# A third shared-expert product ahead of the output projection, and a one-column copy behind the expert choice

## The chip, the cores and the metric

The kernel runs on one core of one Trainium2 chip. The metric is device time in microseconds (us) of one execution. A core has TensorE (PE, matrix products; its weight loads are shown apart as PEld), VectorE (DVE), ScalarE (ACT), GpSimd (POOL) and SyncE (SP), each with an instruction stream of its own that runs strictly in order. Engines wait for each other only through semaphores.

## The reference, cut to what matters

4096 tokens of 256 channels go through an RWKV block and then through a layer of experts.

```
xk, xv, xr = xn*mix + shift(xn)*(1-mix)          # xn: layer norm, shift: one token back
k, v, r    = xk@Wk.T, xv@Wv.T, xr@Wr.T
x   = x + (sigmoid(r) * wkv(k, v)) @ Wo.T        # wkv: running sums over the tokens
xn2 = layer_norm(x); xk2, xr2 = mixed and shifted likewise
x   = x + sigmoid(xr2@Wr_ffn.T) * (relu(xk2@Wk_ffn.T)**2 @ Wv_ffn.T)
...
idx = argmax(xf @ Wg)                            # one of 8 experts for each token
out = geglu(xf, w1s, w2s, w3s) + geglu(xf, W1[idx], W2[idx], W3[idx])
```

`geglu(x, a, b, c)` is `(gelu(x@a) * (x@b)) @ c` with 1024 inner channels. Layer norms and residual sums stand around both parts.

## The kernel before, in words

The tokens go through in 16 chunks of 256. `chunk_steps` runs a software pipeline: step `i` works on chunk `c0 = i` (time mix: k, v, r, the scans, the output projection), `c1 = i-1` (channel mix), `c2 = i-2` (shared expert and expert choice), `c3 = i-3` (shared expert's down projection, placing and sending the rows), and prepares the inputs of chunk `i+1`. Steps -1 to 5 are written out, steps 6 to 13 come from a loop of two steps a turn, steps 14 to 17 are written out again. After them a second phase, `slot_steps`, takes the tokens sorted by expert in slots of 128; the change does not touch it.

What sets the order inside a step is the order in which each engine's `step` function calls its helpers (all in `build`). Four places matter here.

**TensorE's `step`** (lines 588 to 618) ends with `channel_mix_down(0..3)`, `output()`, `shared_gate(2)`, `shared_up(2)`, `shared_gate(3)`, `shared_up(3)`; the next step opens with `projection(0)`, `projection(1)`, `transpose_normed2()`. `output()` (L562) waits for `rw`, the product `val*er` that VectorE writes in L1099. `shared_gate(g)` forms `xf@w1s` for a quarter of the inner channels in PSUM bank `up[(3+2g)%4]`; for `g = 2` it waits for the split of `xf` and for `relu_up(0)`. Each shared product, and each of the three projections, is `channel_major`: 12 half-precision products of 256 columns (a value is split in a high and a low half, and `three` at L342 to L344 adds three partial products). The fp32 products (L546, L549, L562) are each recorded as two instructions.

**VectorE's `step`**, in its middle: `shared(0)`, `shared(1)` (L1207, each waits for ScalarE and for `shared_up`), in every odd step the low half of an expert's weights (`late_lo`, L983), `den_old`, `num_old`, `den_now` (L1070, L1089, L1074), then `halo` (L1002), `own(0)`, `gate` (L1154 to L1162), then `den_r` (L1079), `num` (L1094), `mix0` (L1012), `divide` (L1084), `rw` (L1099).
- `halo(xnT, i+1, ...)` copies the last token's column of this chunk's `xnT` in front of the next chunk's. It waits for ScalarE's `xnT_norm` (L663), and GpSimd's `delta_of` (L1507) waits for it.
- `own(0)` does anything in step 2 alone: the low half of the last weight piece (L977, 2048 elements a partition).
- `gate(c2)` takes the 8 logits of each token, their maximum and its index, casts the index and compares it to get a one-hot row.
- `mix0` needs `delta`, so it waits for GpSimd.

**GpSimd's `step`** runs `delta_of()`, then `mix_lo(0)`, `mix_lo(1)` (L1560), `sh_lo(0)` (L1554), `scatter(c3)` (two indirect DMAs), `sh_lo(1)`, `mix_lo(2)`, `inverse2()` and `inverse1()` (L1466 to L1476). `mix_lo(m)` waits for ScalarE's `mix_hi(m)` (L785), which waits for `mix0(m)`.

**The way from the output projection to the next step:** `x2_sum` (L1106, waits for `output()`), `x3_moments` and `x2_moments` (L989, L992) on VectorE, `inverse2` and `inverse1` on GpSimd, `ln2` on ScalarE (L669, behind `gelu(3)`, a table load and `sh_hi(2)`), and then `transpose_normed2()` on TensorE (L351).

Of the kernel before, what the change touches and what calls it, by code (L numbers as in the profile page):

```python
# [38 lines left out]
def wait(eng, sem, value):  # L39


    if not isinstance(value, int) or value > 0:
        eng.wait_ge(sem, value)


def build(nc, a):
    ctx = ExitStack()
    with ctx:
        def sb(name, shape, dt=F32):
            return ctx.enter_context(nc.sbuf_tensor(name, [P] + list(shape), dt))  # L50
# [6 lines left out]
        def S(name):  # L57
            if name not in sems:
                sems[name] = ctx.enter_context(nc.semaphore(name))
            return sems[name]  # L60
# [45 lines left out]
        xnT = [sb(f"xnT{b}", [CT, CH + 1]) for b in range(2)]  # L106
# [121 lines left out]
        def on(c):  # L228

            return not isinstance(c, int) or 0 <= c < NC  # L230

        def at_step(i, n):
            return isinstance(i, int) and i == n
# [113 lines left out]
        def _(pe):  # L347
# [55 lines left out]
            def step(i, p, h):  # L403
# [67 lines left out]
                def shared_of(g, mat, bank, done):  # L471
                    channel_major(bank, lambda j, s, k: shared_w[:, mat, s, k * F + (2 * g + j) * P:
                                                                 k * F + (2 * g + j + 1) * P], xf_s, done)

                def shared_gate(g):
                    if not on(c2):
                        return
                    if at_step(i, 2) and g == 0:
                        pe.wait_ge(S("piece_lo"), NEEDS_SHARED)
                    wait(pe, S("xf_lo"), c2 + 1)  # L480

                    if g >= 2:
                        if on(c1):
                            wait(pe, S("relu"), 4 * c1 + 2 * g - 3)
                        else:
                            wait(pe, S("gelu"), PAIRS * c2 + g - 1)
                    elif g == 0:
                        if on(c2 - 1):
                            wait(pe, S("gelu"), PAIRS * c2 - 1)
                        else:  # L490
                            wait(pe, S("relu"), 4 * c1 - 3)
                    elif on(c0):
                        wait(pe, S("val"), c0 + 1)
                    else:
                        wait(pe, S("gelu"), PAIRS * c2)
                    shared_of(g, 0, up[(3 + 2 * g) % 4], "sh_gate_mm")

                def shared_up(g):
                    if not on(c2):
                        return  # L500

                    if g >= 2:
                        if on(c1):
                            wait(pe, S("relu"), 4 * c1 + 2 * g - 2)
                        else:
                            wait(pe, S("gu"), PAIRS * c2 + g - 1)
                    elif on(c0):
                        wait(pe, S(("dist", "er")[g]), c0 + 1)
                    else:
                        wait(pe, S("gu"), PAIRS * c2 + g - 1)  # L510
                    shared_of(g, 1, up[(4 + 2 * g) % 4], "sh_up_mm")
# [25 lines left out]
                def channel_mix_down(q):  # L537
                    if not on(c1):
                        return
                    if at_step(i, 1) and q == 0:  # L540
                        pe.wait_ge(S("fv_in"), 16)
                    if q == 0:
                        wait(pe, S("y_sh"), c1 - 1)
                    wait(pe, S("kf"), 4 * c1 + q + 1)
                    for f in (2 * q, 2 * q + 1):
                        pe.matmul(yp[1][:, 0, :], kf[:, f, 0:P], w_fv[:, f, :], start=(f == 0), stop=(f == FT - 1))  # L546
                    if q == 3:
                        for f in range(FT):
                            m = pe.matmul(yp[1][:, 1, :], kf[:, f, P:CH], w_fv[:, f, :], start=(f == 0),  # L549
                                          stop=(f == FT - 1))  # L550
                        m.then_inc(S("fv_mm"), 1)

                def output():
                    if not on(c0):
                        return
                    if at_step(i, 0):
                        pe.wait_ge(S("o_in"), 16)
                    wait(pe, S("rw"), c0 + 1)
                    wait(pe, S("sig"), c0)
                    for t in range(TT):  # L560
                        for k in range(CT):
                            m = pe.matmul(yp[0][:, t, :], val[:, k, t * P:(t + 1) * P], w_o[:, k, :], start=(k == 0),  # L562
                                          stop=(k == CT - 1))
                    m.then_inc(S("wo_mm"), 1)
# [46 lines left out]
                    ranks(c2)  # L611
                for q in range(4):
                    channel_mix_down(q)
                output()
                shared_gate(2)
                shared_up(2)
                shared_gate(3)
                shared_up(3)
# [3 lines left out]
                if at_step(i, NC) or at_step(i, NC + 1):  # L622
                    for q in range(PAIRS + 1):
                        shared_down(c2, q)

            chunk_steps(pe, step)

            pe.wait_ge(S("y_sh"), NC)
# [331 lines left out]
        def _(dve):  # L960
            def held(sem, value):

                wait(dve, sem, value)
                if not isinstance(value, int):
                    dve.memset(hold_dve[:], 0.0)
# [32 lines left out]
            def halo(buf, c, b, done, norm):  # L998

                wait(dve, S(norm), CT * (c + 1))  # L1000
                last = 0 if isinstance(c, int) and c == 0 else CH
                dve.tensor_copy(buf[b][:, :, 0:1], buf[1 - b][:, :, last:last + 1]).then_inc(S(done), 1)  # L1002
# [69 lines left out]
            def den_now(c):  # L1072
                wait(dve, S("denominator"), 4 * c + 1)
                dve.tensor_tensor(den[:], den[:], ex[:, E_NOW], ALU.add).then_inc(S("denominator"), 1)  # L1074

            def den_r(c):
                wait(dve, S("denominator"), 4 * c + 2)
                wait(dve, S("er"), c + 1)
                dve.scalar_tensor_tensor(out=er[:], in0=er[:], scalar=1.0, in1=den[:], op0=ALU.add,  # L1079
                                         op1=ALU.mult).then_inc(S("denominator"), 1)  # L1080
# [10 lines left out]
            def num(c):  # L1091
                wait(dve, S("old"), c + 1)
                wait(dve, S("now"), c + 1)
                dve.tensor_tensor(val[:], now[:], dist[:], ALU.add).then_inc(S("num"), 1)  # L1094
# [53 lines left out]
            def gate(c):  # L1148

                CHOICE = 2 * TT + 1  # L1150
                logit = tp[0][:, 0, 0:TT * E].rearrange("p (t e) -> p t e", t=TT)
                held(S("gate_mm"), c + 1)
                for t in range(TT):
                    dve.max(best[:, t, :], logit[:, t, :]).then_inc(S("choice"), 1)  # L1154
                held(S("choice"), CHOICE * c + TT)
                for t in range(TT):
                    dve.max_index(best_at[:, t, :], best[:, t, :], logit[:, t, :]).then_inc(S("choice"), 1)
                wait(dve, S("choice"), CHOICE * c + 2 * TT)
                dve.tensor_copy(best_f[:], best_at[:, :, 0]).then_inc(S("choice"), 1)
                wait(dve, S("choice"), CHOICE * (c + 1))  # L1160
                for t in range(TT):
                    dve.tensor_scalar(onehot[:, t, :], iota_e[:], best_f[:, t:t + 1], None,  # L1162
                                      ALU.is_equal).then_inc(S("onehot"), 1)
# [36 lines left out]
            def step(i, p, h):  # L1200
# [15 lines left out]
                def own(part):  # L1216
                    for n in own_pieces(OWN_LO, i, part):
                        own_lo(n)
# [57 lines left out]
                if on(c0):  # L1276
                    den_old(c0)
                    num_old(c0)
                    den_now(c0)
                if on(i + 1):  # L1280
                    halo(xnT, i + 1, 1 - p, "halo", "xnT")
                own(0)
                if on(c2) and not at_step(i, NC + 1):
                    gate(c2)
                if on(c0):
                    den_r(c0)
                    num(c0)
# [99 lines left out]
            def last_slots():  # L1387
# [13 lines left out]
                dve.tensor_copy(slot_expert[:], slot_f[:, EXPERT, :]).then_inc(S("slot_table"), 1)  # L1401

            chunk_steps(dve, step)

            def slot_step(j, b, h):
# [284 lines left out]
```

## Time and profile before

| | |
|---|---|
| time, median of 3 runs | 1024.32 us (1023.39 to 1027.34) |
| the profiled execution's own time | 1025.26 us |
| its span | 1023.5 us |
| PE busy | 932.7 us, 91% |
| DVE busy | 719.4 us, 70% |
| ACT busy | 587.0 us, 57% |
| POOL busy | 587.9 us, 57% |
| granted TensorE clock, mean | 0.97 |
| two steps of the middle of the chunk phase | 75.2 us (output projections at 301.68 and 376.84) |

An instruction's row gives its start and duration in microseconds from the start of the span, and in brackets how long its engine had been idle before it and what ended that. Busy shares are means over stages with different limits: in the chunk phase (up to about 660 us) VectorE is busy some nine tenths of the time, in the slot phase it is less. The ends of matmuls are modelled, and matmuls overlap, so that distances between their starts say more than their durations.

### The profile page before, as it was taken

The page shows a single profiled execution, that of the slowest core. Times are in us where ns is not written, and L with a number is a line of the kernel's source. Part 1 is how long each engine was busy: PE and PEld are TensorE (multiplying, and loading weights), DVE is VectorE, ACT ScalarE, POOL GpSimd, SP SyncE. Part 2 cuts the span into 40 slices and gives each one's busy share as a digit, 9 for nine tenths or more (in the row PEclk, how much of TensorE's full clock was granted, in tenths as well). Part 3 has the DMA queues.
Part 4 walks back from the last instruction along what each step waited for, and adds up shares of the span by engine and source line. Part 5 has one row for each costly group of instructions (what it writes and reads, how often), then busy time and mean ns, then how long its engine had stood idle before and what let it go on. Part 6 is the DMA issues. An engine that isn't in the chain of part 4 may idle for free.

```text
span 1023.5 us, 28050 instructions
## 1 busy us (share of the span) xinstructions
PE 932.7 (91%) x9734; PEld 839.7 (82%) x9734; DVE 719.4 (70%) x1653; ACT 587.0 (57%) x1014; POOL 587.9 (57%) x800
## 2 busy tenths in 40 slices
PE   2387899999999999999999999779999999999994
PEld 1266789888888888888888878568999999999994
DVE  6988898998998998998998984513444444444442
ACT  5477677778768868868868755223333333333331
POOL 5446567767766766866866542434445554545553
PEclk9688999999999999999999999889999999999998
DMA  7113151351352252152161268375886788476510
GB/s 236 62 53 112 44 185 50 118 206 34 113 208 56 88 205 81 63 212 96 41 231 68 84 206 285 135 238 194 289 263 216 238 271 261 154 257 195 183 54 22
DMA packets 87338, 156.36 MB, mean 153 GB/s; under 512 B 5549, under 2 KB 68142, under 8 KB 82160
## 3 DMA queue, kind: packets, MB, share of 16 engines
q1 hardware_dynamic: 35760, 72.74, 20.8%
q10 hardware_dynamic: 46960, 65.89, 19.9%
q0 software_dynamic: 4560, 16.98, 4.3%
q8 instruction: 33, 0.54, 0.2%
q14 instruction: 25, 0.20, 0.1%
HBM read 178.35 MB, written 50.51 MB: 224 GB/s over the span
## 4 chain that ended last, share of the span: by engine, by line
PE 60%; DVE 17%; issue 8%; ACTq 6%; ACT 4%; POOL 2%; DMA 2%; DVEq 0%; POOLq 0%
PE up L342 12%; PE up L344 12%; PE up L343 12%; PE yp L342 6%; PE yp L343 6%; PE yp L344 6%; DVE er L1084 5%; PE yp L562 3%; ACTq L881 2%; DVE mixed L1012 2%; PE tp L351 1%; DVE arena L983 1%; DVE val L1099 1%; ACTq L901 1%; ACTq L884 1%
## 5 line engine op out<-in xcount | busy, mean ns | idle before, releaser
L342 PE MATMUL up<-mix_s,arena 128*128 128x128 f16 x1248 | 211.2, 219 | 3.6 <-DVE ex L1426 2.1
L343 PE MATMUL up<-mix_s,arena 128*128 128x128 f16 x1248 | 211.1, 219 | 0.0
L344 PE MATMUL up<-mix_s,arena 128*128 128x128 f16 x1248 | 211.1, 219 | 0.0
L342 PE MATMUL up<-xf_s,arena 128*128 128x256 f16 x512 | 140.3, 274 | 3.4 <-issue 2.4
L1655 POOL TENSOR_TENSOR kf_s<-ex,kf_s 128x512 f16<-128x512 f32 x78 | 90.2, 1156 | 88.5 <-ACT kf_s L942 88.4
L343 PE MATMUL up<-xf_s,arena 128*128 128x256 f16 x512 | 140.4, 274 | 0.0
L344 PE MATMUL up<-xf_s,arena 128*128 128x256 f16 x512 | 140.3, 274 | 0.0
L1426 DVE SCALAR_TENSOR_TENSOR ex<-up,ex 128x512 f32<-128x512 f32 x78 | 53.9, 691 | 105.0 <-ACT ex L936 104.7
L342 PEld LDWEIGHTS up<-mix_s,arena 128*128 128x128 f16 x1248 | 122.1, 98 | 5.3 <-DVE ex L1426 3.4
L343 PEld LDWEIGHTS up<-mix_s,arena 128*128 128x128 f16 x1248 | 122.1, 98 | 0.4
L344 PEld LDWEIGHTS up<-mix_s,arena 128*128 128x128 f16 x1248 | 122.1, 98 | 0.0
L1554 POOL TENSOR_TENSOR sh_s<-gu,sh_s 128x512 f16<-128x512 f32 x64 | 76.6, 1198 | 57.2 <-ACT sh_s L778 56.9
L936 ACT ACTIVATE ex<-up 128x512 f32<-128x512 f32 x78 | 45.9, 589 | 104.5 <-issue 54.0
L942 ACT ACTIVATE kf_s<-ex 128x512 f16<-128x512 f32 x78 | 49.1, 630 | 80.8 <-DVE ex L1426 68.7
L1560 POOL TENSOR_TENSOR mix_s<-mixed,mix_s 128x512 f16<-128x512 f32 x48 | 57.9, 1222 | 55.7 <-ACT mix_s L785 55.7
L342 PE MATMUL yp<-arena,kf_s 128*128 128x256 f16 x312 | 85.0, 273 | 0.8 <-issue 0.7
L343 PE MATMUL yp<-arena,kf_s 128*128 128x256 f16 x312 | 85.0, 273 | 0.0
L344 PE MATMUL yp<-arena,kf_s 128*128 128x256 f16 x312 | 85.0, 273 | 0.0
L342 PE MATMUL yp<-arena,sh_s 128*128 128x256 f16 x256 | 72.8, 284 | 10.4 <-POOL sh_s L1554 10.4
L771 ACT ACTIVATE gu<-up 128x512 f32<-128x512 f32 x64 | 36.8, 596 | 69.8 <-PE up L344 60.2
L343 PE MATMUL yp<-arena,sh_s 128*128 128x256 f16 x256 | 72.8, 284 | 0.0
L344 PE MATMUL yp<-arena,sh_s 128*128 128x256 f16 x256 | 72.5, 283 | 0.0
(228 smaller groups left out, 2893.8 us busy)
## 6 DMA issues: line engine op xcount, KB each, us to landing
arena<-w_split ACTq DMA_DIRECT2D x117, 1024.0 KB
arena<-in_W SPq DMA_DIRECT2D x24, 1024.0 KB, 6.2
w_split<-arena SPq DMA_DIRECT2D x24, 1024.0 KB, 9.1
rows<-routed_rows ACTq DMA_DIRECT2D x39, 261.0 KB, 2.9
routed_rows<-x_in SPq DMA_DIRECT2D x8, 650.0 KB, 6.3
normed<-routed_rows ACTq DMA_DIRECT2D x39, 128.0 KB, 2.5
x_in<-in_x SPq DMA_DIRECT2D x16, 256.0 KB, 2.8
x_res<-in_x SPq DMA_DIRECT2D x16, 256.0 KB, 2.8
```

The source lines that it names most:

```text
L342: pe.matmul(out, stat(0), mov(0), start=first, stop=False)
L343: pe.matmul(out, stat(0), mov(1), start=False, stop=False)
L344: return pe.matmul(out, stat(1), mov(0), start=False, stop=last)
L562: m = pe.matmul(yp[0][:, t, :], val[:, k, t * P:(t + 1) * P], w_o[:, k, :], start=(k == 0), stop=(k == CT - 1))
L771: act.activation(gu[g % GUS][:], up[(3 + 2 * g) % 4][:], ACT.Gelu, scale=1 / WS).then_inc(S("gelu"), 1)
L936: act.activation(slot_g[q], up[2 * q][:].rearrange("p k n -> p (k n)"), ACT.Gelu, scale=1 / WS).then_inc(S("slot_gelu"), 1)
L942: act.activation(slot_h[b][:, 0, q * FT // 2:(q + 1) * FT // 2, :], slot_g[q].rearrange("p (f n) -> p f n", n=P), ACT.Copy).then_inc(S("sl ...
L1084: dve.reciprocal(er[:], er[:]).then_inc(S("denominator"), 1)
L1426: dve.scalar_tensor_tensor(out=slot_g[q], in0=up[2 * q + 1][:].rearrange("p k n -> p (k n)"), scalar=HS / WS, in1=slot_g[q], op0=ALU.mult, ...
L1554: pool.tensor_tensor(sh_s[:, 1, 2 * g:2 * g + 2, :], gu[g % GUS][:], sh_s[:, 0, 2 * g:2 * g + 2, :], ALU.subtract).then_inc(S("sh_lo"), 1)
L1560: pool.tensor_tensor(mix_s[m][:, 1], mixed[m][:], mix_s[m][:, 0], ALU.subtract).then_inc(S("mix_lo"), 1)
L1655: pool.tensor_tensor(hs[:, 1], slot_g[q].rearrange("p (f n) -> p f n", n=P), hs[:, 0], ALU.subtract).then_inc(S("slot_h_lo"), 1)
```

## The change

On TensorE, `shared_gate(2)` moves from behind `output()` to ahead of it, in every step. On VectorE, `gate(c2)` and step 2's `own(0)` now come ahead of the `halo` of the next chunk. No instruction is added or removed, and the waits of the moved parts keep their values.

```diff
@@ TensorE, step
                 for q in range(4):
                     channel_mix_down(q)
+                shared_gate(2)
                 output()
-                shared_gate(2)
                 shared_up(2)
                 shared_gate(3)
                 shared_up(3)
@@ VectorE, step
                     den_now(c0)
-                if on(i + 1):
-                    halo(xnT, i + 1, 1 - p, "halo", "xnT")
                 own(0)
                 if on(c2) and not at_step(i, NC + 1):
                     gate(c2)
+                if on(i + 1):
+                    halo(xnT, i + 1, 1 - p, "halo", "xnT")
                 if on(c0):
                     den_r(c0)
                     num(c0)
```

On TensorE, at the end of a step (`yp<-w_o,val` is the output projection, `up<-xf_s,arena` a shared product; one group of three of the four stands for all):

```order
 L549 MATMUL yp<-w_fv,kf_s 128x256 x8
+L342 MATMUL up<-xf_s,arena 128x256
+L343 MATMUL up<-xf_s,arena 128x256
+L344 MATMUL up<-xf_s,arena 128x256
...
 L562 MATMUL yp<-w_o,val 128x256 x4
-L342 MATMUL up<-xf_s,arena 128x256
-L343 MATMUL up<-xf_s,arena 128x256
-L344 MATMUL up<-xf_s,arena 128x256
```

Twelve products now stand between the channel mix's last product and the output projection; as many fewer follow it before the next step.

On VectorE, in the middle of step 3 (`xnT<-xnT` is the halo's copy, `er<-er,mixed` is `den_r`):

```order
 L1089 TENSOR_TENSOR dist<-ex,state 128x512
 L1074 TENSOR_TENSOR mixed<-mixed,ex 128x512
-L1002 COPY xnT<-xnT 128x2
-L1154 MAX best<-tp 128x8 x2
-L1157 MAX_INDEX best_at<-best,tp 128x8 x2
-L1159 CAST best_f<-best_at 128x2
-L1162 TENSOR_SCALAR onehot<-iota_e,best_f 128x8 x2
+L1154 MAX best<-tp 128x8 x2
+L1157 MAX_INDEX best_at<-best,tp 128x8 x2
+L1159 CAST best_f<-best_at 128x2
+L1162 TENSOR_SCALAR onehot<-iota_e,best_f 128x8 x2
+L1002 COPY xnT<-xnT 128x2
 L1079 SCALAR_TENSOR_TENSOR er<-er,mixed 128x512
 L1094 TENSOR_TENSOR val<-mixed,dist 128x512
```

The copy now has two products of two SBUF tensors right behind it, where it had the small operations of the choice. In step 2 the weight split moves ahead of the copy as well:

```order
 L1074 TENSOR_TENSOR mixed<-mixed,ex 128x512
-L1002 COPY xnT<-xnT 128x2
 L977 SCALAR_TENSOR_TENSOR arena<-arena 128x2048
 L1154 MAX best<-tp 128x8 x2
```

There the copy stands behind both.

## Rows read from the trace of the kernel before

**Rows 1.** Waits of the whole span: us in total, times, longest.

```profile
PE yp L562 <- DVE val L1099: 21.5, 15, 10.4
```

**Rows 2.** TensorE in time around an output projection, an odd step (7).

```profile
293.81 3.62 PE L546 MATMUL yp<-w_fv,kf_s 128*128 128x256 f32 x16
297.27 3.62 PE L549 MATMUL yp<-w_fv,kf_s 128*128 128x256 f32 x16
301.68 1.99 PE L562 MATMUL yp<-w_o,val 128*128 128x256 f32 x8 [0.79 <-DVE val L1099]
...
311.38 0.65 PE L351 MATMUL tp<-ident,normed 128*128 128x128 f32 x4
```

**Rows 3.** The same in the even step behind it (8).

```profile
335.02 3.62 PE L549 MATMUL yp<-w_fv,kf_s 128*128 128x256 f32 x16
339.17 1.99 PE L562 MATMUL yp<-w_o,val 128*128 128x256 f32 x8 [0.54 <-DVE val L1099]
...
348.86 0.60 PE L351 MATMUL tp<-ident,normed 128*128 128x128 f32 x4
```

**Rows 4.** VectorE in time, odd step.

```profile
288.40 0.69 DVE L1207 SCALAR_TENSOR_TENSOR gu<-up,gu 128x512 f32<-128x512 f32 x1 [0.86 <-PE up L344]
...
293.02 0.16 DVE L1002 COPY xnT<-xnT 128x2 f32<-128x2 f32 x1
...
293.79 0.61 DVE L1159 CAST best_f<-best_at 128x2 f32<-128x2 uint32 x1
...
294.71 0.68 DVE L1079 SCALAR_TENSOR_TENSOR er<-er,mixed 128x512 f32<-128x512 f32 x1
...
295.92 1.67 DVE L1012 SCALAR_TENSOR_TENSOR mixed<-delta,vec,xnT 128x256 f32<-128x256 f32 x4
...
305.62 0.15 DVE L992 BATCH_NORM_AGGREGATE mv<-stats 128x2 f32<-128x6 f32 x1
```

**Rows 5.** VectorE in time, even step.

```profile
330.51 0.17 DVE L1002 COPY xnT<-xnT 128x2 f32<-128x2 f32 x1 [1.86 <-ACT xnT L663]
...
333.42 1.67 DVE L1012 SCALAR_TENSOR_TENSOR mixed<-delta,vec,xnT 128x256 f32<-128x256 f32 x4
```

**Rows 6.** GpSimd in time, odd step.

```profile
293.34 1.04 POOL L1507 TENSOR_TENSOR delta<-xnT 128x512 f32<-128x512 f32 x1 [4.47 <-DVE xnT L1002]
297.53 2.28 POOL L1560 TENSOR_TENSOR mix_s<-mixed,mix_s 128x512 f16<-128x512 f32 x2 [3.15 <-ACT mix_s L785]
...
306.08 0.20 POOL L1466 TENSOR_TENSOR inv<-mv,eps_ws 128x2 f32<-128x2 f32 x1
...
308.95 0.20 POOL L1476 TENSOR_TENSOR inv<-inv 128x2 f32<-128x2 f32 x1
```

**Rows 7.** ScalarE in time, odd step: ln2.

```profile
310.18 1.08 ACT L669 ACTIVATE normed<-x,inv 128x256 f32<-128x256 f32 x2
```

**Rows 8.** VectorE in time, step 15, where no halo stands ahead of the choice.

```profile
593.44 0.24 DVE L1154 MAX8 best<-tp 128x8 f32<-128x8 f32 x2
...
594.13 0.17 DVE L1159 CAST best_f<-best_at 128x2 f32<-128x2 uint32 x1
...
594.60 0.68 DVE L1079 SCALAR_TENSOR_TENSOR er<-er,mixed 128x512 f32<-128x512 f32 x1
```

**Rows 9.** GpSimd and VectorE in time where a small GpSimd operation lasts long.

```profile
318.14 4.16 POOL L1480 TENSOR_TENSOR inv<-inv,mv 128x2 f32<-128x2 f32 x1
...
321.56 0.68 DVE L1051 TENSOR_TENSOR dist<-ex,val 128x512 f32<-128x512 f32 x1
```

**Rows 10.** TensorE in time, step 2.

```profile
105.19 3.62 PE L549 MATMUL yp<-w_fv,kf_s 128*128 128x256 f32 x16
112.13 3.39 PE L562 MATMUL yp<-w_o,val 128*128 128x256 f32 x8 [3.33 <-DVE val L1099]
```

**Rows 11.** VectorE in time, step 2.

```profile
100.42 0.17 DVE L1002 COPY xnT<-xnT 128x2 f32<-128x2 f32 x1 [1.60 <-ACT xnT L663]
...
105.42 1.67 DVE L1012 SCALAR_TENSOR_TENSOR mixed<-delta,vec,xnT 128x256 f32<-128x256 f32 x4
```

## The prediction

> **What bounds the kernel now.** I began with TensorE's waits over the whole span. The row to see is the output projection waiting for VectorE's `val` (`rw`): 21.5 us in 15 waits [rows 1]. The longest, 10.4 us, is in step 0, where no shared product exists yet that could fill it; step 2 has 3.33 us [rows 10]; the rest, some 7.8 us, is spread over the twelve steps 3 to 14. Then I read TensorE in order of time around one such wait in each kind of step. Groups of 16 fp32 instructions follow each other at 3.46 us (293.81 to 297.27), so after the last group the next product could start at 297.27 + 3.46 = 300.73. It starts at 301.68: a **hole of 0.95 us** in the odd step [rows 2]. In the even step the same reckoning gives 338.48 against 339.17, **0.69 us** [rows 3]. TensorE has nothing else to wait for in these steps. So the chunk phase is bound by TensorE, plus this hole, whose length VectorE sets.
>
> VectorE itself is anchored to TensorE: it waits 0.86 us for `shared_up(1)` at 288.40 in the odd step [rows 4]. From there to `rw` it runs without a pause. In the even step it also waits 1.86 us at the halo for ScalarE's `xnT` [rows 5].
>
> **TensorE's part: twelve products into the hole.** A half-precision product of 256 columns takes a new place every 0.109 us: from the projection's start to the transposes there are 9.70 us (301.68 to 311.38 [rows 2]; 9.69 in [rows 3]), 72 products and the projection's own 1.83. Twelve are 1.31 us. After the change the projection can start 1.31 us after the free place and is followed by 9.70 - 1.31 = 8.39 us of work up to the transposes. If `rw` is ready by then, the whole hole goes: 0.95 us in an odd step, 0.69 in an even one. The data of the moved products (`xf`'s split, bank 3 after `relu_up(0)`) are old by then. Switching once more between fp32 and half precision I cost at nothing: from the half-precision products to the fp32 transposes the row shows no gap beyond the usual one.
>
> **VectorE's part: when is `rw` ready?** Before, the halo stands at 293.02, `delta` runs on GpSimd from 293.34 for 1.04 us beside the choice, `den_r` starts at 294.71 and `mix0` at 295.92 [rows 4, 6]. From halo to `delta` there are 0.32 us. The choice takes 1.61 us there (0.08 after the halo's start to 294.71), of which the cast is 0.61, and the cast ends at 294.40, just as `delta` does (294.38). In step 15, with no `delta` beside it, the choice takes 594.60 - 593.44 = 1.16 us and the cast 0.17 [rows 8]. So the cast waits for GpSimd, and moved ahead of the halo it won't.
>
> Now `delta` starts beside `den_r` and `num`, which both read two tensors from SBUF. What that does is bounded by two rows. Below, nothing: `delta` takes 1.04 us as now. Above, exclusion: a GpSimd operation on two numbers lasts from 318.14 to 322.30, 0.06 us after VectorE's product of two SBUF tensors that starts at 321.56 has ended [rows 9]. I take exclusion, because that row has the same kinds of operands. Then in an odd step:
> - choice 293.02 to 294.18, halo, `den_r` from 294.26 and `num` for 1.28 us in all, to 295.54. `delta` could start at 294.50, but gets through only then: to about 296.55.
> - `mix0` at 296.62 in place of 295.92: **0.70 us later**, and `rw` with it. It is ready 0.95 + 0.70 = 1.65 us after TensorE's free place; the moved products cover 1.31; a hole of 0.34 stays, and TensorE gains 0.61.
>
> The Trainium skill (page "SBUF — State Buffer", section "Who interferes with whom") has the rule: a VectorE instruction with two SBUF inputs and a GpSimd instruction that reads SBUF exclude each other, and whoever starts first keeps the port for the whole instruction. By its wording `delta` would slip in between `den_r` and `num`, where my row shows no slipping in; `mix0` would come out at 296.6 either way, so the sum is the same by both, and it speaks against this half of the change.
>
> In an even step the halo goes on waiting for `xnT` at 330.51, the choice fills that wait, `num` ends at 331.87 and `delta` about 332.9, some 0.5 us ahead of the 333.42 of before [rows 5]. `rw` is ready well before 1.31; TensorE gains its 0.69.
>
> **What is late next: the normed rows of the next step.** The projection comes later against TensorE's other work, and its result must go through VectorE's sums and moments, GpSimd's `inverse2` and `inverse1` and ScalarE's `ln2` before the transposes at 311.38, which have no slack: `ln2` ends at 311.26 [rows 2, 7]. But `ln2` now waits for ScalarE's own queue, which hangs on `shared_gate(3)` and so moves with TensorE: `inverse1` ends at 309.15 and `ln2` starts at 310.18 [rows 6, 7]. Less 0.08 for the signal, the slack is 0.95 us.
> - Odd step: ScalarE comes 0.61 us earlier. GpSimd's queue, which runs on from `mix_lo(0)` at 297.53 to `inverse2` at 306.08 and hangs on `mix0` [rows 6], comes 0.70 later. 1.31 - 0.95 = 0.36 short; gain 0.61 - 0.36 = **0.25 us**.
> - Even step: ScalarE 0.69 earlier; the projection 1.31 - 0.69 = 0.62 later. GpSimd's queue isn't late here; the moments were ready 0.31 us before `inverse2` began (305.77 against 306.08 [rows 4, 6], taken for the even step too) and 0.08 go to the signal, so `inverse2` starts 0.39 later. 1.08 - 0.95 = 0.13 short; gain **0.56 us**.
>
> Six pairs of steps, 3 to 14: 6 x 0.81 = **4.9 us**. A check on the size: the holes of [rows 2, 3] average 0.67 us by the waits' own count, the whole row 7.8/12 = 0.65.
>
> **Step 2.** Free place at 105.19 + 3.46 = 108.65, projection at 112.13: a hole of 3.48 us [rows 10]. VectorE was done at 100.42 - 1.60 = 98.82 and now does the weight split (2.20, 100.50 to 102.70 by the next instruction's start) and the choice (1.16) while it waited: halo 102.18, `num` to 103.46, `delta` to 104.5, `mix0` at 104.57 in place of 105.42 [rows 11]: 0.85 earlier. With 1.31 fewer behind the projection that is 2.16, less 0.13 as above. The projection took 3.39 us there and 1.99 elsewhere [rows 10, 2]: after this hole TensorE ran at the lower of its two clock levels. The new hole is 1.3 us, between one that leaves the clock alone (0.95) and one that does not (3.48); I take half of the 1.40. Together **2.7 us**.
>
> Steps 0 and 1 have no moved product, step 15 has no hole (its projection follows at once) and no halo, and nothing in the second phase is touched: 0. The halo's later place costs nothing to anyone but `delta`.
>
> Sum: 4.9 + 2.7 = 7.6 us off. Against the profiled execution, 1025.26 - 7.6 = 1017.7; that execution is 0.94 above the median of the runs shown, so 1024.3 - 7.6 = **1016.7 us**.
>
> **Rivals**, each by the same steps:
> - **No exclusion.** `delta` takes 1.04 us beside `den_r`. `mix0` comes 0.27 us earlier in odd steps; TensorE gains 0.95 - 0.13 = 0.82 there; pairs 8.3 us. Step 2: `mix0` at 103.6, 1.8 earlier, all the clock's 1.4 back: 4.5. About 1011.5 us. For it: nothing. Against it: the 4.16 us of [rows 9]. 0.10.
> - **The choice doesn't get shorter** (something else than `delta` held the cast): `mix0` 1.15 us later in odd steps, TensorE 0.16 earlier, 0.36 short: a loss of 0.20; pairs 6 x 0.36 = 2.2, step 2 about 2.2: 1019.9 us, no change that can be told. Against it: the matching ends. 0.18.
> - **The hole moves.** The slack of 0.95 us is not there and the wait for `rw` is paid again as a wait for the normed rows; step 2 alone gains: 1021.6 us. For it: the transposes start 0.12 us after `ln2` ends. 0.09.
> - **Slower: GpSimd's `inverse1` is held.** Later by 0.4 to 0.7 us, it falls deeper beside VectorE's `x1_sum`, two instructions of the shape of `mix0`, of which four take 1.67 us [rows 4]: 0.84 us. If its small operations are held that long, `ln2` and the transposes of `normed2` wait as much longer in 13 steps: 13 x 0.84 = 10.9 against the 7.6, 3.3 us slower, 1027.6 us. It turns the sign once the hold is over 7.6/13 = 0.58 us a step, and passes 0.5% at (7.6 + 5.1)/13 = 0.98; the hold of [rows 9], some 4 us, is the bound above. Against it: it stands beside that sum already. 0.07.
>
> **How the numbers follow.** The forecast has 0.56. Its own spread, some 2 us to either side from step 2's clock (0.7) and steps whose holes differ, puts nearly all of it below 1019.2. A measurement of this kernel can tell about 0.5% (5.1 us) from no change. Faster: 0.52 of the forecast and 0.10 of no exclusion, 0.62. Same: 0.34, with a part of the last rival. Slower: 0.04, the rest of it. The range 1011.5 to 1021.8 takes in all but that rival and tails.
>
> **What would show it.** Right: TensorE's waits at L562 in odd steps 0.2 to 0.4 us and none in even ones; the cast at 0.17 to 0.2 us; `delta` in odd steps recorded at about 2 us; two steps in 74.4 us in place of 75.2; small waits of L351 for `normed`. Wrong: `delta` at 1.04 us beside `den_r`, a cast of 0.6, or waits of L351 over 0.7 us a step.

## The result, and the profile after

The changed kernel takes 1010.96 us (median of 4 runs, 1010.42 to 1011.86), the kernel before 1023.86 us in the same comparison (1022.42 to 1027.34): ratio 0.987, 95% interval 0.9857 to 0.9884. That is 12.9 us less where 7.6 were forecast, and 0.5 us outside the range given (1011.5 to 1021.8). Sign and main mechanism were right, several sizes were not.

TensorE's waits over the whole span, after (us in total, times, longest), against the 21.5 us of [rows 1]:

```profile
PE yp L562 <- DVE val L1099: 11.7, 4, 10.4
```

Of the fifteen waits for `rw` four are left: step 0's of 10.4 us, step 2's of 0.96 and two small ones. The same three places in time as in [rows 2] and [rows 3], TensorE after, an odd step (7) and the even one behind it (8); the part between the rows is left out:

```profile
291.35 3.62 PE L549 MATMUL yp<-w_fv,kf_s 128*128 128x256 f32 x16
...
296.15 1.99 PE L562 MATMUL yp<-w_o,val 128*128 128x256 f32 x8
...
304.87 0.65 PE L351 MATMUL tp<-ident,normed 128*128 128x128 f32 x4 [0.18 <-ACT normed L669]
...
328.51 3.62 PE L549 MATMUL yp<-w_fv,kf_s 128*128 128x256 f32 x16
333.27 1.89 PE L562 MATMUL yp<-w_o,val 128*128 128x256 f32 x8
...
341.55 0.60 PE L351 MATMUL tp<-ident,normed 128*128 128x128 f32 x4
```

From one step's last channel-mix group to the next's there are now 37.16 us behind an odd step (before 37.75) and 36.62 behind an even one (365.13 - 328.51; before 37.42). The free place, where the next product could start, is 3.46 us after each L549. In the even step the projection starts 1.30 us after it, the length of the moved products, and the transposes follow 8.28 us later with no wait. In the odd step it starts at 296.15, 1.34 after the place, and the transposes come 10.06 after the place. Without a wait they would come at 9.72: 8.38 us behind a projection that had itself been waited for, as in step 2. That is a wait of 0.34 us for the normed rows, of which the row calls 0.18 idle.

VectorE after, the odd step's middle, against [rows 4]:

```profile
282.49 0.69 DVE L1207 SCALAR_TENSOR_TENSOR gu<-up,gu 128x512 f32<-128x512 f32 x1 [0.87 <-PE up L344]
...
287.80 0.17 DVE L1159 CAST best_f<-best_at 128x2 f32<-128x2 uint32 x1
...
288.28 0.16 DVE L1002 COPY xnT<-xnT 128x2 f32<-128x2 f32 x1
288.35 0.68 DVE L1079 SCALAR_TENSOR_TENSOR er<-er,mixed 128x512 f32<-128x512 f32 x1
288.95 1.53 DVE L1094 TENSOR_TENSOR val<-mixed,dist 128x512 f32<-128x512 f32 x1
290.40 1.66 DVE L1012 SCALAR_TENSOR_TENSOR mixed<-delta,vec,xnT 128x256 f32<-128x256 f32 x4
```

GpSimd and ScalarE after, the same step, against [rows 6] and [rows 7]:

```profile
288.60 1.33 POOL L1507 TENSOR_TENSOR delta<-xnT 128x512 f32<-128x512 f32 x1 [5.66 <-DVE xnT L1002]
...
303.42 0.20 POOL L1476 TENSOR_TENSOR inv<-inv 128x2 f32<-128x2 f32 x1
```

```profile
303.65 1.09 ACT L669 ACTIVATE normed<-x,inv 128x256 f32<-128x256 f32 x2 [0.22 <-POOL inv L1476]
```

The cast takes 0.17 us in all 16 steps. `delta` is recorded at 1.33 us and `num` at 1.53 instead of 0.68: `delta` asked while `den_r` ran, got through when `den_r` ended, and `num` stood until `delta` was done (289.93). `mix0` starts 7.91 us after `shared(1)`, before 7.52: 0.39 us later. And `ln2` in odd steps now waits for `inverse1`, where ScalarE's own queue had bound it.

VectorE after, the even step (8):

```profile
324.00 0.17 DVE L1002 COPY xnT<-xnT 128x2 f32<-128x2 f32 x1 [0.67 <-ACT xnT L663]
...
335.20 0.87 DVE L1106 SCALAR_TENSOR_TENSOR x<-normed,spread,yp 128x256 f32<-128x256 f32 x2 [1.10 <-PE yp L562]
```

The choice has eaten most of the 1.86 us of waiting at the halo [rows 5]. `x2_sum` (L1106) starts 1.93 us after the projection does (335.20 - 333.27).

Step 2, TensorE after, against [rows 10]:

```profile
105.88 3.62 PE L549 MATMUL yp<-w_fv,kf_s 128*128 128x256 f32 x16
111.77 2.00 PE L562 MATMUL yp<-w_o,val 128*128 128x256 f32 x8 [0.96 <-DVE val L1099]
```

Where the time went, from the starts of the rows of L549 in steps 2 and 15, of the second phase's first transposes (L377) and of the last store (L1647), us:

| | before | after | gain |
|---|---|---|---|
| up to step 2's last channel-mix group | 105.19 | 105.88 | -0.69 |
| step 2 to 3 | 41.90 | 37.85 | 4.05 |
| step 3 to 15 (12 intervals) | 450.16 | 442.22 | 7.94 |
| step 15 to the second phase | 74.06 | 74.44 | -0.38 |
| second phase | 343.51 | 340.92 | 2.59 |

The last row belongs to nothing in the change: in the twelve profiles of this study the second phase took 340.2 to 343.5 us, the part before it 72.4 to 75.6, the start 105.2 to 107.4, and none of the three goes with the kernel (three profiles of the changed kernel gave 74.4, 72.6 and 72.5 for the part before the second phase). The stretch from step 2 to step 15 repeats within 0.4 us in three profiles of the same program (480.07, 480.43, 480.04). So I judge the experiments by that stretch, "the chunk stretch", and use the medians as a check.

### The profile page after: what moved, and what is told of

Read it like the earlier page. It is cut to its first block, busy times and chain, and to the rows that moved or that the text cites. A ratio compares the mean times of both kernels' runs of the same rounds, so it can differ in the third digit from the quotient of the medians.

```text
span 1010.0 us, 28050 instructions
## 1 busy us (share of the span) xinstructions
PE 930.1 (92%) x9734; PEld 839.3 (83%) x9734; DVE 722.3 (72%) x1653; ACT 585.6 (58%) x1014; POOL 588.6 (58%) x800
## 4 chain that ended last, share of the span: by engine, by line
PE 69%; DVE 9%; issue 7%; POOL 7%; ACT 3%; DMA 2%; ACTq 1%; POOLq 0%; DVEq 0%
PE up L342 13%; PE up L344 13%; PE up L343 13%; PE yp L342 7%; PE yp L343 6%; PE yp L344 6%; PE yp L546 2%; PE yp L549 2%; PE yp L562 2%; PE tp L351 2%; DVE arena L983 1%; POOL mix_s L1560 1%; DVE er L1084 1%; POOL routed_rows L1595 1%; POOL sh_s L1554 1%
## 5 line engine op out<-in xcount | busy, mean ns | idle before, releaser
L344 PE MATMUL yp<-arena,sh_s 128*128 128x256 f16 x256 | 72.6, 284 | 0.0
```

The lines of the kernel that those rows point to most:

```text
L344: return pe.matmul(out, stat(1), mov(0), start=False, stop=last)
```

## The experiments

**e1: TensorE's half alone.**

```diff
--- before
+                shared_gate(2)
                 output()
-                shared_gate(2)
```

> TensorE's half of the change alone: the third shared gate ahead of the output projection, VectorE as before. Theory A (TensorE's half is nearly all of it, and in odd steps VectorE's half only costs): mix0 keeps its old place, rw is ready 0.95 us (odd) and 0.69 us (even) after TensorE's free place, both under the 1.31 us of the moved products, so both holes close; against the change the odd steps gain up to 0.35 us more each, while step 2 keeps a hole of about 2.2 us and perhaps the lower clock there. 6 x (0.95 + 0.80) = 10.5 us in steps 3 to 14, 1.3 to 2.7 in step 2: 11.5 to 13 us faster than the kernel before, about 1011 to 1012.5 us. Theory B (both halves are needed): with the halo in its old place even steps gain no more than 0.69 and odd ones stay at the change's 0.59, step 2 gives 1.3: about 9 us faster, 1015.

Measured: 1011.24 us, ratio to before 0.9872 (0.9851 to 0.9894). Chunk stretch 480.38 us against 492.06 before and 480.07 with the whole change. Steps 3 to 14: odd ones 36.63 to 36.89, even ones 36.62, both faster than or equal to the whole change. Step 2 to 3 takes 40.59 us, only the 1.31 of the moved products less than before:

```profile
106.82 3.62 PE L549 MATMUL yp<-w_fv,kf_s 128*128 128x256 f32 x16
113.77 3.33 PE L562 MATMUL yp<-w_o,val 128*128 128x256 f32 x8 [2.02 <-DVE val L1099]
```

Theory A holds. TensorE's half alone gives 11.7 of the chunk stretch's 12.0 us. VectorE's half on top of it gives 2.74 us in step 2 and loses 2.43 in the steps behind (442.22 against 439.79), 0.4 in each odd one.

**e2: VectorE's half alone.**

```diff
--- after
-                shared_gate(2)
                 output()
+                shared_gate(2)
```

> VectorE's half alone: choice and own split ahead of the halo, TensorE as before. Theory A: in odd steps mix0 comes 0.39 us later (the changed kernel's rows show it), the hole grows from 0.95 to 1.34 us; in even steps it comes 0.61 us earlier, the hole shrinks from 0.69 to about 0.1; pairs gain 0.2 us, step 2 gains 1.05 and what the clock gives back (up to 1.4). 2 to 4 us faster than the kernel before, 1020 to 1022. Theory B (VectorE's half is worth as much as TensorE's): 6 us or more.

Measured: 1022.38 us, ratio to before 0.9981 (0.9969 to 0.9993). Chunk stretch 489.46, 2.6 less than before, of it 2.73 in step 2. Even steps lose their hole entirely (the projection at +0.00; 36.74), that of odd steps from 7 on grows to 1.60 us and their interval to 38.41. That is more than the 1.34 expected. GpSimd, then VectorE, then TensorE in step 7 of this kernel:

```profile
294.02 1.93 POOL L1507 TENSOR_TENSOR delta<-xnT 128x512 f32<-128x512 f32 x1 [5.67 <-DVE xnT L1002]
```

```profile
294.37 0.68 DVE L1094 TENSOR_TENSOR val<-mixed,dist 128x512 f32<-128x512 f32 x1
296.06 1.67 DVE L1012 SCALAR_TENSOR_TENSOR mixed<-delta,vec,xnT 128x256 f32<-128x256 f32 x4 [1.01 <-POOL delta L1507]
```

```profile
301.82 1.99 PE L562 MATMUL yp<-w_o,val 128*128 128x256 f32 x8 [1.44 <-DVE val L1099]
```

Here `delta` did not slip in between: `num` ran its 0.68 us right behind `den_r` and `delta` was held over both, 1.93 us. The halo, `den_r`, `num` and `delta` start at the same distances as in the changed kernel, to 0.02 us. So the exclusion has two outcomes; what decides between them is not shown. Theory A's sum holds (2.2 us by the medians, 2.6 by the stretch), though the hole of odd steps grew by 0.65 us where 0.39 were expected.

**e3: halo ahead of the choice in odd steps, behind it in even ones.**

```diff
--- after
+                if on(i + 1) and p == 1:
+                    halo(xnT, i + 1, 1 - p, "halo", "xnT")
                 own(0)
                 if on(c2) and not at_step(i, NC + 1):
                     gate(c2)
-                if on(i + 1):
+                if on(i + 1) and p == 0:
                     halo(xnT, i + 1, 1 - p, "halo", "xnT")
```

> The changed kernel, but in odd steps the halo is back ahead of the choice; even steps (step 2 too) keep it behind. Theory A (the halo behind the choice costs in odd steps, because GpSimd's delta and VectorE's num exclude each other and GpSimd's queue behind it is late for inverse1): the wait for the normed rows at the transposes of odd-to-even steps (0.34 us) goes, six or seven of them: 2 us faster than the changed kernel, about 1009. Theory B (it costs nothing, since the moved products cover it): same as the changed kernel within 0.5 us, 1011.

Measured: 1011.71 us, ratio to before 0.987 (0.9849 to 0.9891), chunk stretch 477.75: 2.3 us below the changed kernel's. TensorE in step 7:

```profile
290.82 3.62 PE L549 MATMUL yp<-w_fv,kf_s 128*128 128x256 f32 x16
...
303.98 0.65 PE L351 MATMUL tp<-ident,normed 128*128 128x128 f32 x4
```

The transposes stand 9.70 us after the free place (290.82 + 3.46) in place of 10.06. `mix0` is back at its old place, 0.39 us earlier, and GpSimd's `inverse1` and the transposes come earlier by as much. Some 0.1 us of the wait is left: the transposes are 8.39 us behind the projection here, 8.28 in even steps. The stretch agrees with theory A, the median by itself did not show it, so it was run again (e10).

**e4: `shared_up(2)` ahead of the projection too.**

```diff
--- after
                 shared_gate(2)
-                output()
                 shared_up(2)
+                output()
```

> The changed kernel with shared_up(2) ahead of the output projection too, 24 products in place of 12. Theory A (the way from the projection through x2, the moments, inverse1 and ln2 to the next transposes has hardly any slack left): the projection comes 1.31 us later against TensorE's other work, ScalarE's ln2 can't start before inverse1, and each step waits at the transposes: 0.34 + 1.31 = 1.6 us in odd steps, about 1.1 in even ones, less what shared_up(2) had waited for: 12 steps, 13 to 16 us slower than the changed kernel, about 1025. Theory B (the slack is 0.95 us or more): 6 us slower or less.

Measured: 1023.78 us, ratio to before 0.9999 (0.9986 to 1.0012): the whole gain is gone. Chunk stretch 490.72, 10.65 more than the changed kernel's; intervals 37.87 behind odd steps (0.7 more) and 37.80 behind even ones (1.2 more). TensorE in step 7:

```profile
299.93 1.89 PE L562 MATMUL yp<-w_o,val 128*128 128x256 f32 x8
308.10 0.65 PE L351 MATMUL tp<-ident,normed 128*128 128x128 f32 x4
```

`ln2` waits 0.98 us for `inverse1` here, in odd and even steps, so this is the way from the projection to the normed rows at its bare length: 8.17 us, and 8.09 in the even step behind it. TensorE's own work on that way is 8.28 us after the change (the even step above) and 1.31 less here. So the changed kernel sits 0.1 to 0.2 us short of the point where the next product moved ahead costs its full length. This is nearer to A (13 to 16 us) than to B (6 or less): 10.65 us by the stretch, 12.8 by the medians. `delta` was held over both VectorE products in five of this kernel's six odd steps (1.93 us in step 7), as in e2.

**e5: the changed kernel again**, unedited.

> The changed kernel once more, unedited: is the way in which delta and num share the port in odd steps the same in another execution, and how much do the second phase and the start vary? Theory A (the outcome is fixed by the program's timing): delta 1.33 us and num 1.53 us in every odd step, intervals of 37.15 and 36.62 us between the last channel-mix products again, the chunk phase within 0.5 us of the first execution, the time about 1011, differences between executions in the start and the second phase alone (up to 3 us). Theory B (it falls either way by chance): some odd steps with delta at 1.93 and num at 0.68 us, whose intervals are about 0.3 us longer.

Measured: 1010.39 us, ratio 0.9884 (0.9866 to 0.9901), chunk stretch 480.43. All odd steps fall as before but one, step 5. GpSimd and VectorE there:

```profile
215.08 2.02 POOL L1507 TENSOR_TENSOR delta<-xnT 128x512 f32<-128x512 f32 x1 [5.92 <-DVE xnT L1002]
```

```profile
215.51 0.68 DVE L1094 TENSOR_TENSOR val<-mixed,dist 128x512 f32<-128x512 f32 x1
```

In the first execution that `delta` took 1.41 us and `num` 1.52. So the program alone doesn't fix the outcome: the same step of the same program falls either way, and it costs 0.27 us in that step (37.61 against 37.34). Mostly A, in one step B.

**e6: `den_r` ahead of the halo.**

```diff
--- after
+                if on(c0):
+                    den_r(c0)
                 if on(i + 1):
                     halo(xnT, i + 1, 1 - p, "halo", "xnT")
                 if on(c0):
-                    den_r(c0)
                     num(c0)
```

> The changed kernel with den_r ahead of the halo, so that num alone stands beside delta. Theory A (the port passes at an instruction's boundary): delta asks 0.32 us after the halo, when num has begun, and gets through when num ends: recorded at about 1.4 us, num at 0.68; mix0 comes 0.26 us later than in the changed kernel's odd steps, the projection starts 1.6 us after TensorE's free place there in place of 1.34; even steps, where the halo waits for xnT anyway, don't change. 1.5 to 2 us slower than the changed kernel. Theory B (two-input instructions keep the port as a run): delta runs when the run ends, as late as it would with both behind the halo: mix0 0.3 us later; the two differ by delta's length only. Theory C (no exclusion between these): delta 1.04 us, mix0 0.06 us earlier.

Measured: 1014.78 us, ratio to before 0.9919 (0.9901 to 0.9937); chunk stretch 481.85, 1.4 to 1.8 more than the changed kernel's. VectorE and GpSimd, step 7:

```profile
290.54 0.16 DVE L1002 COPY xnT<-xnT 128x2 f32<-128x2 f32 x1
290.61 0.69 DVE L1094 TENSOR_TENSOR val<-mixed,dist 128x512 f32<-128x512 f32 x1
292.31 1.67 DVE L1012 SCALAR_TENSOR_TENSOR mixed<-delta,vec,xnT 128x256 f32<-128x256 f32 x4 [1.01 <-POOL delta L1508]
```

```profile
290.87 1.33 POOL L1508 TENSOR_TENSOR delta<-xnT 128x512 f32<-128x512 f32 x1 [6.25 <-DVE xnT L1002]
```

`num` keeps its 0.69 us, `delta` is held until it ends and then takes the rest; `mix0` follows the halo by 1.77 us and the projection stands at +1.6 in odd steps (1.9 in step 5), as theory A had it. Even steps don't move. The median lies further off (3.8 us) than the stretch explains. The part from step 15 to the second phase took 1.7 us more here than in e5, but no more than in the changed kernel's first profile, so the rest is open.

**e7: step 2's weight split behind the halo.**

```diff
--- after
-                own(0)
                 if on(c2) and not at_step(i, NC + 1):
                     gate(c2)
                 if on(i + 1):
                     halo(xnT, i + 1, 1 - p, "halo", "xnT")
+                own(0)
```

> The changed kernel with step 2's weight split behind the halo again, the choice still ahead of it. Only step 2 can change. Theory A (the split ahead of the halo fills the wait for xnT, 1.6 us, which the choice fills by 1.2): in step 2 mix0 comes 0.6 to 0.9 us later than in the changed kernel (delta held beside the split), the projection starts about 3.2 us after TensorE's free place in place of 2.43, TensorE's hole grows to 1.9 us; if the clock stays up 0.8 us slower than the changed kernel, if it falls 2 us slower. All other steps the same. Theory B (the choice alone fills it): no difference in step 2.

Measured: 1010.9 us, ratio 0.9886 (0.987 to 0.9903). Step 2 to 3 takes 38.24 us, 0.39 more; the projection starts at +2.82. TensorE's hole is longer, and the clock stays up: windows of this kernel (stretch, us, busy by engine, PEclk, DMA):

```profile
108.00:116.00 8.00, 6.65 (x41) 5.48 (x40) 7.79 (x9) 6.48 (x8) 5.64 (x5) 1.00 0.00 0
```

Half of theory A's price: `delta` is recorded at 3.01 us beside the split, but `mix0` comes only 0.40 us later against TensorE than in the changed kernel, where 0.6 to 0.9 were expected. Moving the split ahead is worth 0.4 us, once.

**e8: `den_r` and `num` ahead of the halo**, so that `delta` runs beside nothing.

```diff
--- after
-                if on(i + 1):
-                    halo(xnT, i + 1, 1 - p, "halo", "xnT")
                 if on(c0):
                     den_r(c0)
                     num(c0)
+                if on(i + 1):
+                    halo(xnT, i + 1, 1 - p, "halo", "xnT")
```

> The changed kernel with den_r and num both ahead of the halo: nothing with two SBUF inputs stands beside delta. Theory A (exclusion costs 0.3 us in odd steps, and taking it away by waiting costs more than it gives): delta 1.04 us, num 0.68, mix0 0.53 us later than in the changed kernel's odd steps, the projection 1.87 us after the free place there; even steps unchanged or 0.3 us later in mix0, hidden; 3 to 4 us slower than the changed kernel. Theory B (the shared port is the larger cost): no slower.

Measured: 1013.41 us, ratio 0.9913 (0.9896 to 0.993), chunk stretch 483.73, 3.3 to 3.7 more than the changed kernel's; odd steps 37.5 to 37.8, the projection at +1.92 in most of them. GpSimd, step 7:

```profile
290.97 1.04 POOL L1507 TENSOR_TENSOR delta<-xnT 128x512 f32<-128x512 f32 x1 [6.88 <-DVE xnT L1002]
```

With neither product beside it `delta` is back at 1.04 us. So the 1.33 to 2.02 of the other kernels come from the two products. Waiting them out costs more than running beside them. The medians show 2.5 us of it, the stretch 3.3 to 3.7.

**e9 and e10: the changed kernel and e3's, side by side on one chip.**

> The changed kernel, to stand beside the next one on the same chip: about 1010.7 us; chunk phase 480.1 to 480.5 us from step 2's to step 15's last channel-mix products.

> Halo ahead of the choice in odd steps, behind it in even ones. In its first run this stretch took 477.75 us against the changed kernel's 480.07 in its own, but the medians of runs on different chips or hours did not show the 2.3 us. Theory A (the gain is real and was hidden by what varies in the start and the second phase): the stretch again 477.7 to 477.9 us, the median 1 to 3 us below the changed kernel's beside it. Theory B (it is given back behind the chunk phase): the stretch as before, the medians equal within 0.5 us, and the part behind step 15 longer by as much.

Measured: 1011.48 us (1009.35 to 1012.85) and 1009.13 us (1008.26 to 1010.89), ratios to before 0.9872 (0.9854 to 0.9891) and 0.9854 (0.9838 to 0.9871). Chunk stretches 480.04 and 477.71. The 2.3 us are real in the stretch and of that size in these medians too, but the intervals of the two ratios overlap, so the medians alone would not prove it. Theory B of e10 is not quite out: its profile took 2.1 us more from step 15 to the second phase (74.57 against 72.46), as theory B had it. The changed kernel took 74.44 there in its first profile, too, and 72.55 in e5, e3's order 74.49 in its first: two profiles of this order don't settle whether the longer part belongs to it. By the stretch, this is the best version of this study.

## Why the prediction was right and wrong

**TensorE's half: right, and nearly all of it.** The moved products fill the hole where `rw` comes within their 1.31 us. In even steps the projection starts at +1.30, and e1 shows the half alone to give 11.7 us.

**VectorE's part, the cast: right.** 0.61 us to 0.17; `delta` beside it was what stretched it. e3 shows both in one kernel: 0.54 to 0.61 us in the odd steps, where the halo stands ahead of the choice, and 0.17 in the even ones.

**VectorE's part, odd steps: mis-sized, and the largest part of the miss.** "`mix0` at 296.62 in place of 295.92: **0.70 us later**." It was 0.39. The step that failed is the sentence after the rule: that `mix0` would come out the same whether `delta` slips in between `den_r` and `num` or waits for both. It doesn't: when `delta` slips in, only `num` follows it (`mix0` 2.12 us after the halo); when it waits, `delta` itself is last (2.37 in e5's step 5). The Trainium skill's wording (page "SBUF — State Buffer", section "Who interferes with whom"), that the one who starts first keeps the port for that instruction, is what every step of the changed kernel's first profile does, and all but one of e5's; the long hold that I took from [rows 9] is what e2's odd steps 5 to 13 do, where the projection stood 0.65 us later, close to the 0.70. The remaining hole was thus 0.03 us, not 0.34.

The trace before had the nearer row, and I overlooked it. In step 1 there is no choice yet, so the two products stand right behind the halo, as they do in every step after the change. VectorE, then GpSimd, in step 1 of the kernel before:

```profile
64.89 0.17 DVE L1002 COPY xnT<-xnT 128x2 f32<-128x2 f32 x1 [2.51 <-ACT xnT L663]
64.97 0.69 DVE L1079 SCALAR_TENSOR_TENSOR er<-er,mixed 128x512 f32<-128x512 f32 x1
65.58 1.53 DVE L1094 TENSOR_TENSOR val<-mixed,dist 128x512 f32<-128x512 f32 x1
67.03 1.66 DVE L1012 SCALAR_TENSOR_TENSOR mixed<-delta,vec,xnT 128x256 f32<-128x256 f32 x4
```

```profile
65.14 1.43 POOL L1507 TENSOR_TENSOR delta<-xnT 128x512 f32<-128x512 f32 x1 [5.74 <-DVE xnT L1002]
```

`delta` slips in and `mix0` follows the halo by 2.14 us. With a halo at 294.18 that puts `mix0` at 296.32, 0.40 us later than before, and leaves a hole of 0.04: what was measured.

**The way to the normed rows: right in odd steps, too short a slack in even ones.** In odd steps 0.36 us were forecast and 0.34 came, for the reason given: GpSimd's queue hangs on `mix0`. e3 takes that reason away, and all but 0.1 us of the wait goes. In even steps I expected 0.13 and there was none. I had let the moments, and so `x2_sum`, come as much later as the projection. `x2_sum` stood 2.28 us behind it in the trace before (339.17 [rows 3] to 341.45), but there VectorE's own queue held it, and its bare distance is 1.93. Also, a projection that doesn't wait takes 1.89 us instead of 1.99. So the even step 8 gave 0.80 us, not 0.56, and the odd step 7 gave 0.59, not 0.25.

By kind of step, in the chunk stretch: the six odd steps gave 3.53 us where 1.5 were forecast, the six even ones 4.41 where 3.4 were, step 2 4.05 where 2.7 were. Together 12.0 against 7.6.

**Step 2: the mechanism right, the clock's part halved for caution.** 4.05 us against 2.7. VectorE's half brought `rw` 1.05 us nearer (0.85 forecast), and the clock came back whole: the projection took 2.00 us in place of 3.39, and the granted clock from 108 to 116 us was 1.00 in place of 0.79. The clock's part was 1.69 us where 0.70 were forecast: from the projection to the transposes, less the 1.31 of the moved products, there had been 10.07 us and were now 8.38.

**Outside the stretch** the profiles differ by another 1.5 us (2.59 in the second phase, less 0.69 and 0.38 ahead of it) that belong to no term and are within what these parts vary by. The stretch's 12.0 us off 1024.3 would have given 1012.3, inside the range, with the sizes off all the same.

**The rivals.** The number of "no exclusion" (1011.5) came closest, by accident: its mechanism is refuted by `delta` at 1.33 us beside the two products and 1.04 without them (e8). "The hole moves" happens in part, 0.34 us in odd steps. "The choice doesn't get shorter" did not happen. `inverse1` was not held: from its first operation (L1466) to its end it took 1.77 us in step 7 before and after. Of the signs named, the cast, the waits for the normed rows and the even steps came as written; `delta` at about 2 us and a wait of 0.2 to 0.4 us at the projection of odd steps did not.

## What to carry to other kernels

Work moved ahead of a waiting product gains at most the length of the wait. What is moved beyond that makes the product later and uses up the slack of what hangs on it further on; once that is gone, it costs its full length. Here the changed kernel stands 0.1 to 0.2 us short of that point, and twelve more products cost 0.7 us in step 7 and 1.2 in step 8 (e4). Reckon each of a change's parts apart: beside TensorE's half, the VectorE half was a help in step 2 alone and cost 0.4 us in every odd step. Before taking a bound from a far row, look for a step of the same kernel that already has the new order (step 1 here). To judge fractions of a per cent, compare the stretch that the change touches between two fixed instructions, not only the medians.

## What the runs showed of the hardware

- A VectorE product of two SBUF tensors and GpSimd's `delta` exclude each other: `delta` takes 1.04 us without one beside it (e8) and 1.33 to 2.02 with, and it is `num` or `delta` that grows. Whether GpSimd gets in between two such VectorE instructions is not settled by the program: with starts equal to 0.02 us it did (`delta` 1.33, `num` 1.53) in the changed kernel and did not (1.93, 0.68) in e2, and step 5 fell differently in two executions of the same program. Of the 36 odd steps from 3 to 13 with `den_r` right behind the halo (six profiles), it was held over both in 11; in the 48 even steps from 4 to 14 with the same order (eight profiles), where `num` starts 0.69 to 0.79 us after the halo instead of 0.67 or 0.68, it was never.
- A cast of two numbers a partition took 0.54 to 0.62 us beside GpSimd's `delta` (steps 3 to 14 before) and 0.17 without it.
- TensorE's clock in step 2: an idle time of 2.02 us at the projection in e1 came with 3.33 us for it and a granted clock of 0.90 in the eight microseconds behind (116 to 124); an idle time of 2.28 us at the same place in e2 left it at 1.99 us, with a granted clock of 1.00 from 108 on. So the length of the hole alone doesn't tell. Before, 3.33 us idle went with 3.39 us for the projection and a granted clock of 0.79 from 108 to 116.
